# A decoder layer with routed experts: gated rows written to their tokens, against rows kept by slot and gathered

## Chip, cores and metric

The kernel runs on 1 core of one Trainium2 chip. The metric is the device time of a run in microseconds (us); lower is better.

## What is computed

The layer takes 64 sequences of 128 tokens with 256 features (8192 tokens) and applies three residual blocks with a normalization after each: a mixer, a cross attention, and a feed-forward block with routed experts. The change touches only the last one and the routing that prepares it. Cut to what matters:

```python
shared = silu(xf @ sg) * (xf @ su) @ sd                     # every token
top_scores, top_idx = top_k(masked, K)                      # K = 4 of E = 32 experts
gates = softmax(top_scores, axis=-1)
capacity = int(N / E * K * 1.25)                            # 1280 rows per expert
pos = cumsum(onehot, axis=0)[arange(N * K), flat_e] - 1     # place in the expert's list
keep = pos < capacity
h = silu(einsum('ecd,edh->ech', buf, wg)) * einsum('ecd,edh->ech', buf, wu)
out_e = einsum('ech,ehd->ecd', h, wd)
gathered = out_e[flat_e, minimum(pos, capacity - 1)]
contrib = gathered * (flat_g * keep)[:, None]
routed = zeros_like(xf).at[tok].add(contrib)
x = layernorm(x + shared + routed)
```

## The kernel before, in words

Five engines run side by side: TensorE (PE), VectorE (DVE), ScalarE (ACT), GpSimd (POOL), and SyncE (SP), which issues plain transfers. Each runs its own program in order, and semaphores tie them together. There is no scheduler: the order on each engine is the order in which the code is written. The stages follow one another with a barrier between them: `setup_stage`, `mixer_stage`, `attention_stage`, `expert_stage` (tiles `e_`), `combine_stage` (tiles `f_`). Matrix products of the last two stages are split into a high and a low part of each operand, three matmuls for each product (L1207).

**Attention stage.** Sixteen groups of 512 tokens. Behind the attention, DVE chooses four experts for each token and computes `slot_i`, the row of `slot_token` for each (token, choice); pairs beyond capacity get a row out of bounds. POOL scatters the token's number there, 16 indirect transfers to a group (L969), and raises `tok` by 512 for the next one (L976). DVE also keeps gates (`k.gate`) and row numbers (`k.slot`) of all tokens in SBUF. SP fills `expert_rows` in DRAM with zeros, 2560 KB to a group. A list of work items is made at the end: 256 rows of one expert each, 92 of them here.

**Expert stage.** Item w uses buffers w % 2. SP loads the token numbers of item w+2 (`load_tok`, L1292), its gate and up weights (`load_up`), the down weights of w+1 (`load_down`), and then stores the rows of item w-1 into `expert_rows` (`store`, L1313). POOL gathers the 256 input rows of item w+2 with two indirect transfers (`gather`, L1354) and makes the low part of the down weights (`down_low`, L1363). PE runs `up(w)`, the transposes of item w+1 (`turn`, L1394), `down(w-1)`. DVE copies the finished product out of PSUM (`copied`, L1545). Engines walk a loop of 79 rounds of two items and skip the rounds that have none.

**Combine stage.** Sixteen groups of 512 tokens. PE runs `up(g)` (48 matmuls of 512 columns), `turn(g+1)` (8 transposes) and `down(g)` (48 matmuls of 256 columns). `down(g)` waits for the last low part of the hidden rows (L1759). POOL gathers four expert rows for each token, 16 indirect transfers to a group (`fetch`, L1639), and computes the inverse deviation (`rstd`, L1646 and L1648). DVE adds the rows one group later, 16 multiply-adds to a group (`adds`, L1770), and normalizes (L1778 to L1788).

Of the kernel before, what the change touches and what calls it, by code (L numbers as in the profile page):

```python
# [90 lines left out]
def setup_stage(nc, k, dram):  # L91

    with ExitStack() as ctx:
# [12 lines left out]
        with nc.Block() as block:  # L106
# [12 lines left out]
            def _(pool):  # L119
# [17 lines left out]
                pool.iota(k.tok[:], pattern=[[T, TG]], base=0, channel_multiplier=1).then_inc(iot, 1)  # L137
# [400 lines left out]
def attention_stage(nc, k, dram):  # L538
# [6 lines left out]
    with ExitStack() as ctx:  # L545
# [32 lines left out]
        pos, kept, posc = p.sb("pos", [P, TG, K]), p.sb("kept", [P, TG, K]), p.sb("posc", [P, TG, K])  # L578
        base = p.sb("base", [P, TG, K])
        far, slot_i = p.sb("far", [P, TG, K]), p.sb("slot_i", [P, TG, K], I32)  # L580
        blank = p.sb("blank", [RT, (SLOTS + SETW) // RT], I32)
        zero_rdy, filled = p.sem("zero_rdy"), p.sem("filled")
# [15 lines left out]
        posc_rdy, hand_rdy, scattered, tok_rdy = p.sem("posc"), p.sem("hand"), p.sem("scattered"), p.sem("tok")  # L598
# [66 lines left out]
        with nc.Block() as block:  # L665
            @block.sync
            def _(sp):
# [8 lines left out]
                FILLED = SLOTS // NG  # L676

                sp.wait_ge(blank_rdy, 1)
                sp.dma_start(k.slot_tok.rearrange("(p n) a -> p (n a)", p=RT), blank[:]).then_inc(blanked, 16)
                sp.wait_ge(zero_rdy, 1)  # L680

                def store(g):
                    sp.dma_start(k.out_d[bass.ds(g * FILLED, FILLED), :].rearrange("(p n) d -> p n d", p=P),
                                 zero[:, None, :].to_broadcast([P, FILLED // P, D])).then_inc(filled, 16)
# [21 lines left out]
                sp.wait_ge(filled, DMA + 16 * NG)  # L706
                sp.wait_ge(blanked, DMA + 16)
# [188 lines left out]
            def _(pool):  # L896
                pool.memset(zero[:], 0.0).then_inc(zero_rdy, 1)
                begin(pool, xs_rdy, xb_rdy, ve_rdy, rs_rdy, rxs_rdy, nms_rdy, nrm_rdy, tok_rdy, mask_rdy)
                pool.memset(blank[:], 0).then_inc(blank_rdy, 1)
                pool.memset(r_half[:], 0.5).then_inc(half_rdy, 1)  # L900
# [54 lines left out]
                def scatter(r, batches, paced):  # L955


                    for j in batches:
                        if j == 0:
                            pool.wait_ge(slot_rdy, ONE + r + 1)  # L960
                            pool.wait_ge(tok_rdy, ONE + r)
                            pool.wait_ge(blanked, DMA + 16)
# [5 lines left out]
                        for q in range(K):  # L968
                            pool.indirect_dma_start(  # L969
                                k.slot_tok, bass.IndirectOffsetOnAxis(ap=slot_i[:, j, q:q + 1], axis=0),  # L970
                                k.tok[:, j:j + 1], None, bounds_check=SLOTS - 1, oob_is_err=False)\
                                .then_inc(scattered, 16)
                    if TG - 1 in batches:
                        pool.wait_ge(scattered, 16 * TG * K * (r + 1))
                        apart(pool, k.past_pool)
                        pool.tensor_scalar(k.tok[:], k.tok[:], float(GW), None, ALU.add).then_inc(tok_rdy, 1)  # L976
# [38 lines left out]
            def _(dve):  # L1015
                begin(dve, a_out[0], nb_rdy, rden_rdy, n_rdy, h_rdy, stat_rdy, mv_rdy, ot_rdy,
                      step, slot_rdy, posc_rdy, dif_rdy)
# [64 lines left out]
                def place(r):  # L1082
# [7 lines left out]
                    then(dve.tensor_tensor(dif[:], ex[:], er[:, :, None].to_broadcast([P, TG, K]), ALU.mult))  # L1090
# [120 lines left out]
def expert_stage(nc, k, dram):  # L1211
# [3 lines left out]
    with ExitStack() as ctx:  # L1215
# [57 lines left out]
        with nc.Block() as block:  # L1273
            @block.sync
            def _(sp):
# [40 lines left out]
                def item(w, a):  # L1316
# [3 lines left out]
                    if at_least(w, 1):  # L1320
                        store(w - 1, 1 - a)
# [576 lines left out]
```

## Time and profile before

| | |
|---|---|
| median of 3 runs | 2421.14 us (2417.51 to 2422.02) |
| the profiled execution: time, span | 2423.74 us, 2422.2 us |
| busy: PE, DVE, ACT, POOL | 88%, 65%, 50%, 56% |
| expert stage, from the first gather to the last copy | 1139.3 to 2001.9 us |
| combine stage, from its first instruction to the end | 2004.7 to 2422.2 us |

Times in the trace count from the span's start. Busy shares are averages over stages with different limits, so each stage is read by itself. A DMA's issue on SP is short; the time to landing is given apart. "issue" as a reason for idle time means that the profile shows nothing that the engine waited for.

### The profile page before, as it was taken

What the parts mean: (1) busy time and instruction counts of PE and PEld (TensorE: products, weight loads), DVE (VectorE), ACT (ScalarE), POOL (GpSimd) and SP (SyncE); (2) the same over time, 40 slices, a digit from 0 to 9 for tenths busy, and PEclk for the clock granted to TensorE, in tenths of its full rate; (3) what the DMA queues carried; (4) which work ended last, traced back from release to release, by engine and by line L of the source; (5) the groups of instructions that cost most, each with busy time, mean ns of one, the idle gap of its engine ahead of it and who ended that gap; (6) DMA issues with size and microseconds to landing.
All of it is one profiled execution on the core that took longest, in us unless ns stands there. A gap on an engine that the chain in (4) does not pass through costs nothing. (4 is left out here: it accounts for less than half of the span.)

```text
span 2422.2 us, 51520 instructions
## 1 busy us (share of the span) xinstructions
PE 2123.5 (88%) x13848; PEld 1722.7 (71%) x13848; DVE 1574.4 (65%) x3953; ACT 1211.0 (50%) x3430; POOL 1351.9 (56%) x1648
## 2 busy tenths in 40 slices
PE   6999699999999999830999999999999956878884
PEld 3555356666666666530999999999999955777774
DVE  4666335667667666632777777777777743766666
ACT  2555245444455445410777777777777742222221
POOL 3666303456655655555555555555555535777775
PEclk9999899999999999955999999999999987989897
DMA  4000112322411321301666666666667643444343
GB/s 127 33 0 0 46 50 78 98 62 59 117 59 59 107 69 59 101 13 58 209 236 239 237 234 228 237 242 228 238 227 243 238 143 126 132 121 136 119 137 91
DMA packets 240146, 317.12 MB, mean 131 GB/s; under 512 B 38073, under 2 KB 161761, under 8 KB 240098
## 3 DMA queue, kind: packets, MB, share of 16 engines
q1 hardware_dynamic: 210594, 258.19, 31.9%
q0 software_dynamic: 29504, 58.37, 8.2%
q8 instruction: 21, 0.34, 0.1%
q14 instruction: 27, 0.22, 0.0%
HBM read 233.34 MB, written 83.14 MB: 131 GB/s over the span
## 5 line engine op out<-in xcount | busy, mean ns | idle before, releaser
L969 POOL DMA_INDIRECT slot_token<-tok,a_slot_i x256 | 267.9, 1047 | 231.0 <-issue 95.6
L1354 POOL DMA_INDIRECT e_xg<-x_rows,e_tok x188 | 197.4, 1050 | 346.2 <-DMA e_tok<-slot_token 188.1
L1639 POOL DMA_INDIRECT f_row<-expert_rows,f_idx x256 | 273.9, 1070 | 89.9 <-issue 76.7
L1532 DVE TENSOR_TENSOR e_hid<-e_sg,e_u 128x256 f32<-128x256 f32 x368 | 155.1, 421 | 133.3 <-PE e_u L1207 106.7
L1482 ACT ACTIVATE e_sg<-e_g 128x256 f32<-128x256 f32 x368 | 141.2, 384 | 179.6 <-PE e_g L1207 179.6
L852 ACT ACTIVATE a_prob<-a_s,a_ntop 128x128 f32<-128x128 f32 x512 | 180.2, 394 | 0.8 <-DVE a_ntop L1149 0.5
L1730 ACT ACTIVATE f_sg<-f_g 128x512 f32<-128x512 f32 x64 | 38.2, 597 | 222.1 <-PE f_g L1207 222.1
L1363 POOL TENSOR_TENSOR e_wd1l<-e_raw_d,e_wd1h 128x256 fp32r<-128x256 f32 x184 | 130.4, 742 | 30.0 <-ACT e_wd1h L1461 29.8
L1207 PE MATMUL f_d<-f_wdh,f_hth 128*128 128x256 f32 x256 | 85.6, 334 | 63.6 <-DVE f_htl L1759 63.6
L1363 POOL TENSOR_TENSOR e_wd0l<-e_raw_d,e_wd0h 128x256 fp32r<-128x256 f32 x184 | 130.9, 743 | 7.3 <-ACT e_wd0h L1461 6.4
L1207 PE MATMUL e_d<-e_wd1h,e_ht1h 128*128 128x256 f32 x368 | 108.3, 294 | 24.5 <-issue 24.5
L783 PE MATMUL a_o<-a_wo,a_ot 128*128 128x256 f32 x512 | 125.6, 390 | 4.2 <-DVE a_ot L1179 4.2
L736 PE MATMUL a_a<-a_wv,a_ct 96*128 96x512 f32 x256 | 120.9, 606 | 6.9 <-ACT a_rxt L837 5.5
L726 PE MATMUL a_a<-a_xt,a_wq 128*128 128x512 f32 x256 | 122.7, 614 | 0.8 <-ACT a_xt L837 0.8
L732 PE MATMUL a_a<-a_ct,a_wk 96*128 96x512 f32 x256 | 120.5, 605 | 0.0
L852 ACT ACTIVATION_READ_ACCUMULATOR a_prob<-a_s,a_ntop 128x1 f32 x512 | 120.5, 235 | 0.0
L1545 DVE COPY e_out<-e_d 128x512 f32<-128x512 f32 x92 | 63.6, 692 | 87.4 <-PE e_d L1207 87.4
L1133 DVE TENSOR_TENSOR x<-a_o,x 128x256 f32 (+1 forms) x64 | 27.2, 425 | 133.5 <-PE a_o L783 133.5
L1207 PEld LDWEIGHTS f_d<-f_wdh,f_hth 128*128 128x128 f32 x256 | 59.9, 234 | 67.6 <-DVE f_htl L1759 38.7
L1207 PE MATMUL e_d<-e_wd0h,e_ht0h 128*128 128x256 f32 x368 | 107.4, 292 | 0.0
L1770 DVE SCALAR_TENSOR_TENSOR f_res<-f_row,gate,f_res 128x256 f32<-128x256 f32 x256 | 106.6, 480 | 0.1
L783 PEld LDWEIGHTS a_o<-a_wo,a_ot 128*128 128x128 f32 x512 | 95.4, 197 | 15.2 <-DVE a_ot L1179 4.4
(262 smaller groups left out, 7522.9 us busy)
## 6 DMA issues: line engine op xcount, KB each, us to landing
e_raw_g<-in_eg SPq DMA_DIRECT2D x94, 512.0 KB
e_raw_u<-in_eu SPq DMA_DIRECT2D x94, 512.0 KB, 4.2
e_raw_d<-in_ed SPq DMA_DIRECT2D x93, 512.0 KB, 5.0
expert_rows<-a_zero SPq DMA_DIRECT2D x16, 2560.0 KB, 11.8
expert_rows<-e_out SPq DMA_DIRECT2D x92, 256.0 KB, 2.2
x<-in_x SPq DMA_DIRECT2D x16, 512.0 KB, 3.4
x_rows<-x SPq DMA_DIRECT2D x16, 512.0 KB, 3.4
f_xs<-x_rows SPq DMA_DIRECT2D x16, 512.0 KB, 4.8
```

Of the source, the lines that this page charges most:

```text
L726: last = pe.matmul(out[:], wq[:, c, m * P:(m + 1) * P], xt[:, c, :], start=(c == 0), stop=(c == DC - 1))
L732: last = pe.matmul(out[:], wk[:, c, m * P:(m + 1) * P], ct[par][:, c, :], start=(c == 0), stop=(c == 1))
L736: last = pe.matmul(out[:], ct[par][:, c, m * T:(m + 1) * T], wv[:, c, :], start=(c == 0), stop=(c == 1))
L783: last = pe.matmul(bank_o[:, 0:D], ot[:, m, :], wo[:, m, :], start=(m == 0), stop=(m == IC - 1))
L852: last = act.activation(prob[b % 2][:, h, :], bank_s[r][:, m * T:(m + 1) * T], ACT.Exp, bias=ntop[b % 2][:, h:h + 1], accum_out=den[b % 2] ...
L969: pool.indirect_dma_start(k.slot_tok, bass.IndirectOffsetOnAxis(ap=slot_i[:, j, q:q + 1], axis=0), k.tok[:, j:j + 1], None, bounds_check=S ...
L1207: last = pe.matmul(out, a, b, start=(n == 0 and t == 0), stop=(n == len(chunks) - 1 and t == 2))
L1354: pool.indirect_dma_start(xg[a][:, n, :], None, k.x2_d, bass.IndirectOffsetOnAxis(ap=tok[a][:, n:n + 1], axis=0))\
L1363: pool.tensor_tensor(wd[par][1][:, m, :], raw_d[par][:, m, :], wd[par][0][:, m, :].bitcast(F32), ALU.subtract).then_inc(dl_rdy, 1)
L1482: act.activation(sg[m % 2][:], bank_g[m % 2][:, 0:SETW], ACT.Silu).then_inc(sg_rdy, 1)
L1532: dve.tensor_tensor(hid[m % 2][:], sg[m % 2][:], bank_u[m % 2][:, 0:SETW], ALU.mult)\
L1639: pool.indirect_dma_start(row[a][:, j, q, :], None, k.out_d[0:SLOTS, :], bass.IndirectOffsetOnAxis(ap=idx[a][:, j, q:q + 1], axis=0))\
```

## The change

1. An entry of `slot_token` has three numbers: the token, the row `4 * token + choice` of a new DRAM tensor `part_rows`, and the gate's bits. Blank entries point to spare rows. DVE no longer writes `k.gate` and `k.slot`. The wait for `tok_rdy` on DVE stands four operations earlier.
2. In the expert stage DVE scales each row by its gate as it leaves PSUM (`gated`, two operations for one). POOL writes the rows of item w-2 to `part_rows` with two indirect transfers (`put_rows`). SP loads the entries of item w once more (`load_dest`), after the rows of item w-2 have landed, since these used the same buffer. SP no longer stores rows.
3. In the combine stage SP loads the four rows of each token plainly (`fetch_part`, 2 MB to a group). POOL adds them and the input (`parts`, four additions of 128x1024) in place of its 16 gathers. DVE's 16 multiply-adds are gone. PE runs `down(g-1)` in group g, with hidden rows in two buffers. DVE normalizes group g-2 in group g.
4. SP's zeros now fill `part_rows`, 2048 KB to a group, and 256 spare rows of `x2_rows`.

```diff
 # expert stage, SP
-                def store(w, a):
+                def load_dest(w, a, i):
                     start = slots(w)
-                    sp.wait_ge(out_rdy, OUT + NP * (w + 1))
-                    sp.dma_start(k.out_d[bass.ds(start, SETW), :].rearrange("(p n) d -> p n d", n=TI), out[a][:])\
-                        .then_inc(stored[a], 16)
-
-                def item(w, a):
+                    if at_least(i, 1):
+                        sp.wait_ge(put[a], 16 * TI * i)
+                        apart(sp, k.past_sp)
+                    sp.dma_start(dest[a][:], k.slot_tok[bass.ds(start, SETW), :].rearrange("(p n) a -> p n a", n=TI))\
+                        .then_inc(dest_in[a], 16)
+
+                def item(w, a, i):
                     load_tok(w + 2, a)
                     load_up(w + 2, a)
                     load_down(w + 1, 1 - a)
-                    if at_least(w, 1):
-                        store(w - 1, 1 - a)
+                    load_dest(w, a, i)
 # expert stage, POOL
+                def put_rows(w, a):
+                    pool.wait_ge(out_rdy, OUT + TI * (w + 1))
+                    apart(pool, k.past_pool)
+                    for n in range(TI):
+                        pool.indirect_dma_start(k.part_d, bass.IndirectOffsetOnAxis(ap=dest[a][:, n, 1:2], axis=0),
+                                                out[a][:, n, :], None).then_inc(put[a], 16)
+
+                def item(w, a, i):
+                    gather(w + 2, a, i + 1)
+                    if at_least(w, 2):
+                        put_rows(w - 2, a)
+                    down_low(w, a)
 # expert stage, DVE
-                def copied(w, a, i):
...
+                def gated(w, a, i):
+
+                    dve.wait_ge(dest_in[a], DMA + 16 * (i + 1))
+                    gate = dest[a][:].bitcast(F32)
+                    for n in range(TI):
+                        if n % 2 == 0:
+                            dve.wait_ge(d_done, ONE + NP * w + n // 2 + 1)
+                        dve.tensor_scalar(out[a][:, n, :], bank_d[a][0:RT, (n % 2) * D:(n % 2 + 1) * D],
+                                          gate[:, n, 2:3], None, ALU.mult).then_inc(out_rdy, 1)
 # combine stage, SP
+                def group(g, a, i):
+                    if at_least(g, 2):
+                        store(g - 2, a)
+                    if not isinstance(g, int) or g + 2 < NG:
+                        sp.wait_ge(acc_rdy, ONE + 4 * (g + 1))
+                        apart(sp, k.past_sp)
+                        fetch(g + 2, a)
+                        fetch_part(g + 2, a)
 # combine stage, POOL
+                    for n, (out, x, y) in enumerate(((to, part[a][:, :, 0, :], part[a][:, :, 1, :]),
+                                                     (both, part[a][:, :, 2, :], part[a][:, :, 3, :]),
+                                                     (to, to[:], both[:]), (to, to[:], xs[a][:]))):
+                        if n >= 2:
+                            pool.wait_ge(acc_rdy, ONE + 4 * g + n)
+                        pool.tensor_tensor(out[:], x, y, ALU.add).then_inc(acc_rdy, 1)
 # combine stage, PE
+                def group(g, a, i):
+                    up(g)
+                    if not is_last(g):
+                        turn(g + 1, 1 - a, i + a)
+                    if at_least(g, 1):
+                        down(g - 1, 1 - a)
```

SP in the loop of the expert stage, from the end of one item into the next (`e_tok`: token numbers, `e_out`: finished rows, `e_dest`: the entries loaded again, `e_put`: counts rows that have landed in `part_rows`). Before:

```order
L1312 REGISTER_ALU
L1313 ISA [waits e_out]
L1313 DMA expert_rows<-e_out 128x512
L1285 ISA
L1285 TENSOR_LOAD plan
L1285 ISA x2
L1290 ISA
L1292 REGISTER_ALU [waits e_t_done]
L1292 DMA e_tok<-slot_token 128x2
```

And now:

```order
L1321 REGISTER_ALU
L1323 ISA [waits e_put0]
L1323 DMA e_dest<-slot_token 128x6
L1293 ISA
L1293 TENSOR_LOAD plan
L1293 ISA x2
L1298 ISA
L1300 ISA [waits e_t_done]
L1300 DMA e_tok<-slot_token 128x6
```

Ahead of the load of token numbers stood a store that waits for DVE (`e_out`); now there stands a load that waits for rows that POOL has written. `TENSOR_LOAD plan` reads an item's first row from the list of items.

POOL in the same loop, one item (`e_xg`: gathered input rows, `e_wd0l`: low part of the down weights). Before:

```order
L1350 ISA
L1351 ISA [waits e_t_done]
L1354 DMA e_xg<-x_rows,e_tok 128x256 [waits e_tok_in0]
L1354 DMA e_xg<-x_rows,e_tok 128x256
L1362 ISA [waits e_d_done]
L1363 TENSOR_TENSOR e_wd0l<-e_raw_d,e_wd0h 128x256 [waits e_dh]
```

And now:

```order
L1358 ISA
L1359 ISA [waits e_t_done]
L1362 DMA e_xg<-x_rows,e_tok 128x256 [waits e_tok_in0]
L1362 DMA e_xg<-x_rows,e_tok 128x256
L1375 ISA
L1378 DMA part_rows<-e_out,e_dest 41216x256 [waits e_out]
L1378 DMA part_rows<-e_out,e_dest 41216x256
L1370 ISA [waits e_d_done]
L1371 TENSOR_TENSOR e_wd0l<-e_raw_d,e_wd0h 128x256 [waits e_dh]
```

Two indirect writes stand behind the two gathers of the same item, and the gathers still wait for the token numbers that SP loads.

## Rows read from the trace of the kernel before

**Rows 1.** The page's busy time of PE: us, share, instructions.
```profile
PE 2123.5 (88%) x13848; PEld 1722.7 (71%) x13848; DVE 1574.4 (65%) x3953; ACT 1211.0 (50%) x3430; POOL 1351.9 (56%) x1648
```

**Rows 2.** Stretch, length; busy PE, PEld, DVE, ACT, POOL; clock; DMA share; GB/s.
```profile
450.00:700.00 250.00, 244.42 (x1495) 158.20 (x1494) 171.49 (x520) 124.14 (x463) 149.85 (x193) 1.00 0.28 72
1300.00:1500.00 200.00, 200.00 (x1705) 200.00 (x1704) 153.38 (x336) 150.18 (x404) 112.66 (x137) 1.00 0.69 237
2140.00:2240.00 100.00, 80.15 (x413) 70.08 (x412) 67.47 (x164) 23.33 (x41) 75.89 (x78) 0.88 0.43 130
```

**Rows 3.** SP's queue in the expert stage, in order: start, duration, issue.
```profile
1481.33 0.37 SPq L1313 DMA_DIRECT2D expert_rows<-e_out  x1
1482.71 0.35 SPq L1292 DMA_DIRECT2D e_tok<-slot_token  x1
...
1490.25 0.37 SPq L1313 DMA_DIRECT2D expert_rows<-e_out  x1
1492.48 0.36 SPq L1292 DMA_DIRECT2D e_tok<-slot_token  x1
...
1500.56 0.35 SPq L1292 DMA_DIRECT2D e_tok<-slot_token  x1
```

**Rows 4.** POOL in the same stretch, in order; idle before in brackets.
```profile
1485.30 1.43 POOL L1354 DMA_INDIRECT e_xg<-x_rows,e_tok  x1 [2.83 <-issue]
1487.04 1.17 POOL L1354 DMA_INDIRECT e_xg<-x_rows,e_tok  x1 [0.30 <-issue]
1488.22 2.82 POOL L1363 TENSOR_TENSOR e_wd1l<-e_raw_d,e_wd1h 128x256 fp32r<-128x256 f32 x4
1494.98 1.01 POOL L1354 DMA_INDIRECT e_xg<-x_rows,e_tok  x1 [3.94 <-DMA e_tok<-slot_token]
...
1503.08 0.95 POOL L1354 DMA_INDIRECT e_xg<-x_rows,e_tok  x1 [2.76 <-issue]
```

**Rows 5.** The tile `e_xg`: landing of its transfers.
```profile
DMA to landing us min/median/max: 2.7/4.6/6.4
```

**Rows 6.** DMA issues: count, KB each, median us to landing.
```profile
expert_rows<-e_out SPq DMA_DIRECT2D x92, 256.0 KB, 2.2
```

**Rows 7.** POOL at the end of the last scatter, in order.
```profile
1129.25 0.97 POOL L969 DMA_INDIRECT slot_token<-tok,a_slot_i  x1 [0.30 <-issue]
1131.53 0.22 POOL L976 TENSOR_SCALAR tok<-tok 128x4 int32<-128x4 int32 x1 [1.31 <-DMA slot_token<-tok,a_slot_i]
```

**Rows 8.** PE in the combine stage: pieces of the chain and one instruction row.
```profile
2038.50 5.95 PE f_d L1207 x48
2047.23 1.40 PE f_g L1207 x6
2141.82 1.09 PE L1669 MATMUL f_t<-ident,f_xs 128*128 128x128 f32 x8
```

**Rows 9.** POOL in the combine stage at the start of two groups.
```profile
2134.01 0.19 POOL L1633 COPY f_idx<-slot 128x16 int32 x1
...
2158.72 0.19 POOL L1633 COPY f_idx<-slot 128x16 int32 x1
```

**Rows 10.** PE after its wait in the combine stage.
```profile
2147.84 0.58 PE L1207 MATMUL f_d<-f_wdh,f_hth 128*128 128x256 f32 x1 [4.92 <-DVE f_htl L1759]
```

**Rows 11.** The start of the combine stage: ACT and PE.
```profile
2016.66 1.06 ACT L1737 ACTIVATE f_wgh<-f_raw_g 128x1024 fp32r<-128x1024 f32 x1 [45.02 <-DMA f_raw_d<-in_sd]
2022.58 0.79 PE L1207 MATMUL f_g<-f_xth,f_wgh 128*128 128x512 f32 x1 [11.98 <-DVE f_xtl L1754]
```

**Rows 12.** DVE at the end of the span.
```profile
2413.84 1.40 DVE L1778 BATCH_NORM_STATS2 f_stat<-f_res 128x6 f32<-128x256 f32 x4
```

**Rows 13.** POOL's groups: count, busy us, mean ns, idle before.
```profile
L1363 POOL TENSOR_TENSOR e_wd0l<-e_raw_d,e_wd0h 128x256 fp32r<-128x256 f32 x184 | 130.9, 743 | 7.3 <-ACT e_wd0h L1461 6.4
L906 POOL TENSOR_TENSOR x<-x,bout 128x1024 f32 x10 | 23.6, 2359 | 0.0
L1639 POOL DMA_INDIRECT f_row<-expert_rows,f_idx x256 | 273.9, 1070 | 89.9 <-issue 76.7 <-POOL f_idx L1633 13.2
```

More of the change, by code:

```diff
@@ L975, in scatter @@
                         apart(pool, k.past_pool)
-                        pool.tensor_scalar(k.tok[:], k.tok[:], float(GW), None, ALU.add).then_inc(tok_rdy, 1)
+                        for n, step_by in enumerate((GW, GW * K)):
+                            last = pool.tensor_scalar(entry[:, :, :, n], entry[:, :, :, n], float(step_by), None, ALU.add)
+                        last.then_inc(tok_rdy, 1)
                 def around(g):
@@ L1368, in first @@
                     gather(1, 1, 0)
-                    gather(2, 0, 1)
-                    down_low(0, 0)
-                    gather(3, 1, 1)
-                    down_low(1, 1)
+                    item(0, 0, 0)
+                    item(1, 1, 0)
                 def again(i):
-                    gather(2 * i + 2, 0, i + 1)
-                    down_low(2 * i, 0)
-                    gather(2 * i + 3, 1, i + 1)
-                    down_low(2 * i + 1, 1)
+                    item(2 * i, 0, i)
+                    item(2 * i + 1, 1, i)
                 used, last = rounds(pool, first, again)
+                put_rows(last - 1, 0)
+                put_rows(last, 1)
                 pool.wait_ge(x_in[1], 16 * TI * (used + 1))
                 apart(pool, k.past_pool)
+                for a in range(2):
+                    pool.wait_ge(put[a], 16 * TI * used)
+                    apart(pool, k.past_pool)
             @block.tensor
@@ L1592, in combine_stage, with at_least, groups, is_last @@
         sg_rdy, hid_rdy, d_done, sum_rdy = p.sem("sg"), p.sem("h"), p.sem("d_done"), p.sem("sum")
-        add_rdy, stat_rdy, mv_rdy, ve_rdy = p.sem("add"), p.sem("stat"), p.sem("mv"), p.sem("ve")
+        stat_rdy, mv_rdy, ve_rdy = p.sem("stat"), p.sem("mv"), p.sem("ve")
         rs_rdy, res_rdy = p.sem("rs"), p.sem("res")
-        stored = [p.sem(f"stored{i}") for i in range(2)]
         out_d = dram["out"].rearrange("b t d -> t b d")
-        x2_rows = k.x2_d.rearrange("(b t) d -> t b d", t=T)
+        x2_rows = k.x2_d[0:B * T, :].rearrange("(b t) d -> t b d", t=T)
+        part_rows = k.part_d[0:B * T * K, :].rearrange("(b t q) d -> t b (q d)", t=T, q=K)
+        def at_least(g, n):
+            return not isinstance(g, int) or g >= n
+        def groups(eng, group):
+            group(0, 0, 0)
+            group(1, 1, 0)
+            with eng.Fori(1, NG // 2 - 1) as i:
+                group(2 * i, 0, i)
+                group(2 * i + 1, 1, i)
+            group(NG - 2, 0, NG // 2 - 1)
+            group(NG - 1, 1, NG // 2 - 1)
+        def is_last(g):
+            return isinstance(g, int) and g == NG - 1
         with nc.Block() as block:
@@ L1822, in _ @@
                     dve.tensor_tensor(w[1][:], raw[i][:], w[0][:].bitcast(F32), ALU.subtract).then_inc(wl_rdy, 1)
-                turned(0)
-                group(0, 0, 0)
-                group(1, 1, 0)
-                with dve.Fori(1, NG // 2 - 1) as i:
-                    group(2 * i, 0, i)
-                    group(2 * i + 1, 1, i)
-                group(NG - 2, 0, NG // 2 - 1)
-                group(NG - 1, 1, NG // 2 - 1)
-                for q in range(K):
-                    adds(NG - 1, 1, NG // 2 - 1, q)
+                groups(dve, group)
+                moments(NG - 2, 0)
+                normed(NG - 2, 0)
+                summed(NG - 1, 1, NG // 2 - 1)
                 moments(NG - 1, 1)
```

317 lines of the change are left out of this document (148 added, 169 removed).

## The prediction, made before the changed kernel was run

> **What bounds the kernel now.** I read the page first: PE is busy for 88% of the span [rows 1]. That is an average over stages, so the next view is busy time by stretch [rows 2]. In the attention stretch PE works 244.42 of 250 us. In the expert stage it works 200.00 of 200 us at the full granted clock (1.00, 2.4 GHz), with POOL at 112.66 and DVE at 153.38. In the combine stage it works only 80.15 of 100 us at a mean clock of 0.88, with POOL at 75.89 busy us. So PE sets the first two, and something else sets the third.
>
> For the expert stage I want the time of one item. SP's issues repeat once an item: two stores stand 1490.25 - 1481.33 = 8.92 us apart [rows 3]. There are 92 items (the stores' count, [rows 6]).
>
> For the combine stage, POOL starts two successive groups at 2134.01 and 2158.72, 24.71 us apart [rows 9]. Its 16 gathers take 1.07 us each [rows 13] and 0.30 us between two ([rows 4] show such a gap). With `rstd`, the copy and their waits that is the whole period. PE also has a wait of its own there, for the last low part of the hidden rows, 4.92 us before `down` [rows 10], and needs far less: 8 blocks of six matmuls at 1.40, transposes of 1.09 and 5.95 for 48 matmuls of `down` are 18.2 us [rows 8].
>
> **Combine stage, the gain.** POOL's 16 gathers leave; four additions of 128x1024 come. The nearest row has 2.359 us for this shape; the dearest one by element has 0.743 us for 256 columns, so 2.97 us for 1024 [rows 13]. Four are 9.4 to 11.9 us, and with some 3 us for `rstd` and waits POOL needs 12.5 to 15 us of a group. DVE loses 16 multiply-adds. `down(g-1)` needs hidden rows that were finished a group before, so the wait of 4.92 us has nothing to wait for. Loads are 3 MB a group (2 of parts, 0.5 in, 0.5 out): 165 GB/s at 18.2 us, under the 237 GB/s that the expert stage moves [rows 2]. PE therefore becomes the bound, at 18.2 us: 16 groups are 291 us.
>
> The start: the weights have landed at 2016.66 and PE starts at 2022.58 [rows 11]. Now no gathers run beside the weights' load, and the first turned rows (two subtractions on DVE) are made ahead of them. I estimate 4 us less in all, so a start at 2018.5. The slow clock at the start costs some 2.5 us (rows 11 show 0.79 for a first matmul). PE ends at 2018.5 + 291 + 2.5 = 2312. Behind it come the last half of the sum (0.9) and what runs today from the statistics to the end, 2422.2 - 2413.84 = 8.4 us [rows 12]. End: 2321, so **-101 us**.
>
> **Expert stage, the loss.** DVE's two scaled copies for one copy, and POOL's two writes for each item, are small beside idle time: POOL is busy 5.0 us of an item's 8.92 [rows 2] and 2 x 1.3 us more still fit. As busy time the change costs nothing here. What it adds is a closed loop of waits. Follow it through the two orders above:
>
> 1. SP issues the token numbers of w+3. POOL's gather of w+3 starts 2.5 us later: 1482.71 to 1485.30, 1492.48 to 1494.98, 1500.56 to 1503.08 [rows 3, 4].
> 2. Two gathers: 1.74 us from the first to the second [rows 4], 1.3 where nothing disturbs (1.01 and the gap of 0.30), so 1.4; then 1.17 + 0.30 to the next issue, 1.4. Sum 2.8.
> 3. POOL's first write of w-1 stands behind them (its rows have long been ready), 1.3 us to the second.
> 4. SP waits until both have landed, L from the start of the second. No row shows this transfer. Below: the last scatter of 4-byte entries starts at 1129.25 and the wait for it ends at 1131.53, 2.3 us [rows 7]. Above: gathers of such rows land 4.6 us after issue at the median, plus 0.2 for SP: 4.8. Their minimum is 2.7 [rows 5]. The two writes start about 4 us behind the first gather, when the item's weights have nearly landed, so I take a lightly loaded one: **L = 3.0**.
> 5. SP issues `load_dest(w+1)`, and the token numbers of w+4 follow as they follow the store today: 1.38 us within a round, 2.23 across the loop's end (1490.25 to 1492.48) [rows 3]; mean 1.8.
>
> Sum: 2.5 + 2.8 + 1.3 + 3.0 + 1.8 = **11.4 us** for one turn, and each turn makes exactly one item. Before, step 4 was a wait for DVE's copy of the product just finished, and PE's own 8.92 us set the rate. In the loop are also queued: `load_up` and `load_down` behind SP's wait, which PE needs only an item later, and POOL's `down_low` (2.82 us [rows 4]) behind the writes, which is over before the next token numbers land. PE sees about 2.5 us of waits per item, in two parts: for the input rows before `turn`, and for the low down weights before `down`.
>
> SP's wait starts with item 2, so 90 turns: (11.4 - 8.92) x 90 = **+223 us**. With L = 2.3 it is +160, with L = 4.8 +385.
>
> The Trainium skill, page DMA: Bandwidth & Descriptors, section Anatomy of one DMA — SWDGE (gpsimd) path, puts a transfer's cost at 2.0 us plus bytes over 436 GB/s, mostly the receipt from the target memory, behind about 1 us for making the descriptors. For 128 KB that is an estimate of 3.3 us for L, and the sum by it would be 250 in place of 223.
>
> **The seam.** Behind the last product stand two scaled copies, two writes and L in place of a copy and a store that lands in 2.2 us [rows 6]: some +2 us.
>
> **Attention stage.** Scattered entries have 12 bytes in place of 4, in as many transfers. The earlier wait for `tok_rdy` and a second small addition on POOL (0.22 us each, [rows 7]) may hold DVE for parts of a us in a group, against three small operations less. PE is the bound there at 98% and DVE has 171 busy of 250 us [rows 2]: 0, within 5 us. SP's zeros are less (2048 KB for 2560) and hidden either way.
>
> **The sum.** 223 - 101 + 2 = +124 us. The profiled execution took 2423.74 us, 2.6 above the median; on the median of 2421.14 I forecast 2545 us. The bounds of L give 2482 to 2707.
>
> **Rivals.**
> - *The loop hides; faster.* The expert stage keeps 8.92 us an item and only the combine gain remains: 2421 - 101 + 2 = 2322 us. For it speaks POOL's 44% of idle time there. Place: SP's wait for the writes. Price: 90 us for each us of a turn. It decides where the turn comes to 8.92 + 99 / 90 = 10.0 us, so at L = 1.6; the shortest landing in the trace is 2.3. Chance 0.08.
> - *The clock falls.* PE's waits of 1 to 2 us in each item could bring the granted clock down to 1.2 GHz. In the combine stage a wait of 4.92 us stands ahead of matmuls at 0.58 for 256 columns and a mean clock of 0.88 [rows 2, 10]. Wholly at half the clock, an item would cost up to 17.8 us and the run 2421 + 800 - 99 = 3120. Below 11.4 / 8.92, so with up to 28% more PE time, the loop hides it. The waits are shorter than the one that is seen to do it, so 0.05. The Trainium skill, page TensorE: Matmul & The Clock Gate, section HAM oscillation — how this bites in real kernels, describes this for matmul bursts with waits for DMA between them; no row of this stage shows it yet.
> - *The combine stage finds another bound.* POOL's additions, the order store, load, parts on SP, or the load of the inputs for `turn` could hold a group at 20 to 22 us: 30 to 60 us more, 2575 to 2605. It lies within the range; 0.12. The Trainium skill, page GPSIMD Engine Reference, section Specifications, says that GpSimd shares its SBUF interface with VectorE and that DVE instructions with two SBUF inputs contend; by that the additions are dearer, and the 0.743 us row, taken beside such instructions, is the bound used above.
> - *A longer loop*, with writes that land after 4.8 us or more: above 2707; 0.05.
>
> **How the numbers follow.** The loop with L from 2.3 to 4.8 and PE-bound combine has 0.70, the same loop with a slower combine 0.12, a longer loop 0.05, the fallen clock 0.05, the hidden loop 0.08. The range of 2475 to 2710 holds the first two. Only the hidden loop is faster; a result within 0.2% (5 us, about what a measurement of this kernel can tell from no change) needs L near 1.6: 0.01. Faster 0.08, same 0.01, slower 0.91.
>
> **What the changed profile would show.** Right: SP's queue waits for the landing of `part_rows`, its issues of token numbers stand 11.4 us apart on average in the expert stage, PE has two short waits an item, its clock stays near 1.00, and the expert stage is some 220 us longer. In the combine stage PE is busy almost without a break and a group takes 18.2 us. Wrong: issues 8.9 us apart (the loop hides), a landing of the writes far from 3.0, a PE clock well under 1, or groups over 19 us with PE waiting for POOL or for a load.

## Result and profile after: slower, 2546.5 us

The changed kernel took 2546.52 us (median of 4 runs, 2543.96 to 2548.92), and the kernel before 2419.37 us in the same measurement (4 runs, 2417.51 to 2422.02). The ratio is 1.0526, with a 95% interval of 1.0513 to 1.0539. The forecast was 2545 us.

First the page of the changed kernel, busy time of PE, and then busy time by stretch: length, busy PE, PEld, DVE, ACT, POOL, clock, DMA share, GB/s.

```profile
PE 2161.0 (85%) x13848; PEld 1739.8 (68%) x13848; DVE 1656.4 (65%) x3741; ACT 1213.5 (48%) x3430; POOL 1517.8 (60%) x1643
...
450.00:700.00 250.00, 244.37 (x1503) 159.60 (x1503) 167.92 (x494) 125.84 (x468) 154.49 (x201) 1.00 0.21 65
1300.00:1500.00 200.00, 170.61 (x1333) 165.20 (x1332) 149.47 (x278) 118.94 (x316) 135.73 (x141) 0.96 0.54 187
2300.00:2400.00 100.00, 100.00 (x588) 88.65 (x587) 75.41 (x142) 30.63 (x55) 67.23 (x36) 1.00 0.50 178
```

Against [rows 2] the attention stretch stands as it was. In the expert stage PE now idles 15% of the time, and the DMA rate fell from 237 to 187 GB/s. In the combine stage PE has no idle time left. So the two big stages have changed places: PE set the expert stage before, and sets the combine stage now.

SP's queue in the expert stage (start, duration, issue), and then what SP waited for there (us in total, times, longest):

```profile
1490.59 0.35 SPq L1300 DMA_DIRECT2D e_tok<-slot_token  x1
1491.88 0.38 SPq L1307 DMA_DIRECT2D e_raw_g<-in_eg  x1
1492.45 0.38 SPq L1310 DMA_DIRECT2D e_raw_u<-in_eu  x1
1493.75 0.37 SPq L1316 DMA_DIRECT2D e_raw_d<-in_ed  x1
1499.71 0.34 SPq L1323 DMA_DIRECT2D e_dest<-slot_token  x1
1501.07 0.35 SPq L1300 DMA_DIRECT2D e_tok<-slot_token  x1
...
1510.59 0.34 SPq L1323 DMA_DIRECT2D e_dest<-slot_token  x1
1512.42 0.35 SPq L1300 DMA_DIRECT2D e_tok<-slot_token  x1
...
2188.90 0.35 SPq L1300 DMA_DIRECT2D e_tok<-slot_token  x1
...
SPq L60 <- DMA part_rows<-e_out,e_dest: 499.7, 90, 7.0
```

POOL beside it (start, duration, instruction; idle before in brackets):

```profile
1497.04 0.99 POOL L1378 DMA_INDIRECT part_rows<-e_out,e_dest  x1 [0.30 <-issue]
1498.06 4.08 POOL L1371 TENSOR_TENSOR e_wd0l<-e_raw_d,e_wd0h 128x256 fp32r<-128x256 f32 x4
1503.46 0.99 POOL L1362 DMA_INDIRECT e_xg<-x_rows,e_tok  x1 [1.31 <-issue]
1504.75 0.96 POOL L1362 DMA_INDIRECT e_xg<-x_rows,e_tok  x1 [0.30 <-issue]
1506.02 1.01 POOL L1378 DMA_INDIRECT part_rows<-e_out,e_dest  x1 [0.30 <-issue]
1507.33 0.99 POOL L1378 DMA_INDIRECT part_rows<-e_out,e_dest  x1 [0.30 <-issue]
```

One can walk the loop in these rows. Token numbers are issued at 1501.07. The gather starts 2.39 us later, the first write 2.56 after that (1506.02), the second 1.31 later (1507.33), and SP is past its wait 3.26 later (1510.59). The next token numbers follow after 1.83. This turn took 11.35 us, and every part of it starts when the part before it ends. SP waited for the writes 90 times, which is every item but the first two. From the load of item 5's numbers at 1181.63 to the last one at 2188.90 there are 88 items, which is 11.45 us an item.

In the combine stage, POOL at the start of three groups:

```profile
2308.39 0.23 POOL L1684 TENSOR_SCALAR f_ve<-f_mv 128x4 f32<-128x4 f32 x1 [5.15 <-DVE f_mv L1832]
...
2325.92 0.23 POOL L1684 TENSOR_SCALAR f_ve<-f_mv 128x4 f32<-128x4 f32 x1 [5.25 <-DVE f_mv L1832]
...
2327.24 2.53 POOL L1702 TENSOR_TENSOR f_acc<-f_part 128x1024 f32<-128x1024 f32 x1
2329.73 2.84 POOL L1702 TENSOR_TENSOR f_both<-f_part 128x1024 f32<-128x1024 f32 x1
2332.64 2.74 POOL L1702 TENSOR_TENSOR f_acc<-f_acc,f_both 128x1024 f32<-128x1024 f32 x1
2335.46 2.74 POOL L1702 TENSOR_TENSOR f_acc<-f_acc,f_xs 128x1024 f32<-128x1024 f32 x1
2343.46 0.23 POOL L1684 TENSOR_SCALAR f_ve<-f_mv 128x4 f32<-128x4 f32 x1 [5.25 <-DVE f_mv L1832]
```

A group takes 17.53 us against 24.71 in [rows 9], and POOL has over 5 us to spare in each. PE has none; the chain of waits there is PE alone (start, length, piece):

```profile
2311.20 1.36 PE f_g L1213 x6
...
2313.92 0.87 PE f_t L1722 x8
2314.79 5.76 PE f_d L1213 x48
```

By stages: the attention stage ends 1.2 us later (first gather at 1140.5 for 1139.3). From that gather to the combine stage's first instruction (at 2233.2) it is 1092.7 us for 865.4, so +227.3. The combine stage takes 312.9 us for 417.5, so -104.6. Together +123.9, which is the difference of the two spans (2546.1 and 2422.2).

### The profile page after: what moved, and what is told of

Same layout as the page of the kernel before. It is cut to its first block and busy times, and to the rows that moved or that the text cites. A ratio compares the mean times of both kernels' runs of the same rounds, so it can differ in the third digit from the quotient of the medians.

```text
span 2546.1 us, 51191 instructions
## 1 busy us (share of the span) xinstructions
PE 2161.0 (85%) x13848; PEld 1739.8 (68%) x13848; DVE 1656.4 (65%) x3741; ACT 1213.5 (48%) x3430; POOL 1517.8 (60%) x1643
## 5 line engine op out<-in xcount | busy, mean ns | idle before, releaser
L980 POOL DMA_INDIRECT slot_token<-a_entry,a_slot_i x256 | 270.3, 1056 | 245.6 <-issue 95.6
L1378 POOL DMA_INDIRECT part_rows<-e_out,e_dest x184 | 195.0, 1060 | 79.1 <-issue 66.7
L1569 DVE TENSOR_SCALAR e_out<-e_d,e_dest 128x256 f32<-128x256 f32 x184 | 80.3, 478 | 149.2 <-PE e_d L1213 148.5
L1371 POOL TENSOR_TENSOR e_wd0l<-e_raw_d,e_wd0h 128x256 fp32r<-128x256 f32 x184 | 172.4, 965 | 7.7 <-ACT e_wd0h L1483 6.7
L1371 POOL TENSOR_TENSOR e_wd1l<-e_raw_d,e_wd1h 128x256 fp32r<-128x256 f32 x184 | 168.9, 946 | 6.0 <-ACT e_wd1h L1483 4.9
L1544 DVE TENSOR_TENSOR e_ht1l<-e_hid,e_ht1h 128x256 fp32r<-128x256 f32 x184 | 134.7, 753 | 0.0
L1213 PEld LDWEIGHTS e_d<-e_wd0h,e_ht0h 128*128 128x128 f32 x368 | 78.4, 213 | 74.0 <-issue 73.8
L1544 DVE TENSOR_TENSOR e_ht0l<-e_hid,e_ht0h 128x256 fp32r<-128x256 f32 x184 | 123.6, 692 | 0.0
L1213 PE MATMUL e_g<-e_xth,e_wg1h 128*128 128x256 f32 x368 | 106.1, 288 | 19.9 <-DVE e_xtl L1539 19.9
L1213 PEld LDWEIGHTS e_d<-e_wd1h,e_ht1h 128*128 128x128 f32 x368 | 74.0, 201 | 71.1 <-issue 71.0
```

The lines of the kernel that those rows point to most:

```text
L980: pool.indirect_dma_start(k.slot_tok, bass.IndirectOffsetOnAxis(ap=slot_i[:, j, q:q + 1], axis=0), entry[:, j, q, :], None, bounds_check=S ...
L1213: last = pe.matmul(out, a, b, start=(n == 0 and t == 0), stop=(n == len(chunks) - 1 and t == 2))
L1371: pool.tensor_tensor(wd[par][1][:, m, :], raw_d[par][:, m, :], wd[par][0][:, m, :].bitcast(F32), ALU.subtract).then_inc(dl_rdy, 1)
L1378: pool.indirect_dma_start(k.part_d, bass.IndirectOffsetOnAxis(ap=dest[a][:, n, 1:2], axis=0), out[a][:, n, :], None).then_inc(put[a], 16)
L1544: dve.tensor_tensor(ht[a][1][:, m, :], hid[m % 2][:], ht[a][0][:, m, :].bitcast(F32), ALU.subtract).then_inc(hl_rdy, 1)
```

## Experiments

Twelve runs of ten different kernels followed (the kernels before and after among them), in four measurements on three chips, each with its own runs of the kernel before. In the first of them that kernel took 2580.05 us (13 runs, 2570.27 to 2591.89) with a mean clock near 0.917; in the other three it took 2418.65, 2419.97 and 2423.61 us, as in the measurement of the result. No profile of it on that chip exists. It ran unchanged with a profile in two later measurements, on other chips, and took its usual time:

*The kernel before, twice.* 

> The kernel before, unchanged, for its profile beside the experiments: in their measurement it took 2580 us, in the first one 2419. Theory: one stage of it alone is longer, and the changed kernel does not have it. First candidate, its combine stage with 256 indirect gathers on POOL (1.07 us each in the first profile): if they take longer there, the group is over 30 us in place of 24.7, and the stage over 500 us in place of 417. Rival: the expert stage is longer, 10.6 us an item in place of 8.92, by the clock or by its loads. Second rival: all stages are longer by the same share, as a lower clock would make them. If this run takes 2420 us again, the difference is one of the chip or of the moment and stays open.

 Measured: 2420.38 us. 

> The kernel before once more, for its profile beside the runs of this measurement. If it takes some 2580 us as in one measurement before, its stages by stretch say where the 160 us are: in the combine stage alone, by a group over 30 us or a lower clock there, or in the expert stage. If it takes 2419 us, that difference stays open.

 Measured: 2424.98 us. So the 160 us stay open, and ratios of the first measurement are not used below; its kernels are compared with one another and by their periods. The changed kernel itself was not run in that measurement: it took 2546.52 and 2549.31 us in two others.

### Is it the loop? The destinations an item later

Item w's destination entries are loaded at the end of item w+1, so SP waits for writes that were issued an item earlier. DVE needs them only after the product of item w, an item after the old place. Not shown are two small transfers on POOL ahead of the stage, which let the first waits pass.

```diff
...
-                    load_dest(w, a, i)
+                    if at_least(w, 1):
+                        load_dest(w - 1, 1 - a, i if a else i - 1)
...
+                load_dest(last, 1, used - 1)
```

> The changed kernel, with one difference in the expert stage: SP loads the entries of item w-1, not of item w, at the end of its item w, so its wait for landed rows is for writes that POOL issued one item earlier. The work on every engine stays the same, but for two small transfers ahead of the stage. Theory of the closed loop (SP's wait, token numbers, gathers, writes, landing): the turn of about 11.4 us now makes two items, 5.7 us each, PE's 8.92 us set the rate again, the expert stage is about 225 us shorter, and the time is 2320 to 2345 us. Rival, POOL and the transfers are too busy with two writes more in an item: the work is unchanged, so the time stays within 20 us of the changed kernel's 2546.5. Rival, DVE's scaled copies wait for their entries: these now land later, so the time is the same or higher.

Measured: 2357.05 us (2355.1 to 2360.23), some 190 us under the changed kernel as the theory of the loop has it, but 12 us above its range; an item takes 9.09 us. SP's largest wait of this kind in the whole trace (us in total, times, longest) is now for PE's transposes, and none for a landing of `part_rows` is left:

```profile
SPq L60 <- PE e_t L1421: 110.5, 59, 4.9
```

It was run once more:

> The experiment with the destinations loaded an item later, once more, beside a kernel before that takes its usual time. In its profile POOL works without a pause in the expert stage: 1.46 + 1.19 + 1.23 + 1.17 for the four indirect issues, 2.81 for the low parts and some 1.1 between them, 8.98 us an item, and PE needs 8.92. Theory (the loop is open, and POOL's own work is now level with PE): 2350 to 2365 us, 0.97 to 0.98 of the kernel before and 185 to 200 us less than the changed kernel, wherever it runs. Rival: its 2357 us belong to the chip of that measurement, and it takes 2400 us or more.

Measured: 2335.62 us (2334.97 to 2337.92), ratio to the kernel before 0.9644 (0.9622 to 0.9665), and an item takes 8.98 us. That is 14 us under the range expected of this run. The changed kernel took 2549.31 us (below), so one load moved by one item takes 214 us away. That is the whole loss and more. Both kernels write and gather the same rows with the same instructions; but for the two small transfers, only what SP waits for differs. Busy time and clock in the same stretch as above, and POOL:

```profile
1300.00:1500.00 200.00, 200.00 (x1694) 200.00 (x1693) 154.82 (x356) 149.08 (x400) 162.12 (x180) 1.00 0.70 234
...
1491.28 1.46 POOL L1367 DMA_INDIRECT e_xg<-x_rows,e_tok  x1 [0.16 <-issue]
1493.04 1.19 POOL L1367 DMA_INDIRECT e_xg<-x_rows,e_tok  x1 [0.30 <-issue]
1494.54 1.23 POOL L1383 DMA_INDIRECT part_rows<-e_out,e_dest  x1 [0.30 <-issue]
1496.07 1.17 POOL L1383 DMA_INDIRECT part_rows<-e_out,e_dest  x1 [0.30 <-issue]
1497.26 2.82 POOL L1376 TENSOR_TENSOR e_wd1l<-e_raw_d,e_wd1h 128x256 fp32r<-128x256 f32 x4
1500.23 1.48 POOL L1367 DMA_INDIRECT e_xg<-x_rows,e_tok  x1 [0.16 <-issue]
```

PE is at 200 of 200 us again, as in [rows 2]. In this item POOL has no gap longer than 0.30 us: its own work fills it (1491.28 to 1500.23), and of the 3.9 us of an item that it had free before almost nothing is left. Which of the two sets the 8.98 us was not separated. PE has no wait in the trace between 1200 and 1900 us, while POOL waits there 24 times for ACT, 26.0 us in all, which speaks for PE.

### Another way to open it: the writes ahead of the gathers

```diff
-                    gather(w + 2, a, i + 1)
                     if at_least(w, 2):
                         put_rows(w - 2, a)
+                    gather(w + 2, a, i + 1)
```

> The changed kernel, with POOL's two writes of item w-2 ahead of the two gathers of item w+2 in place of behind them. SP's program is unchanged. Theory of the closed loop: the writes no longer stand behind gathers that need the token numbers of the same turn. The chain from one write to the next is 1.3 + 3.3 (landing) + 1.6 (SP) + 2.5 (token numbers) + 2.6 (gathers) + 3 to 4 (low part of the weights), about 14.5 us, for two items, so 7.2 us an item: PE sets the rate, 2320 to 2350 us. Rival, POOL or transfers too busy: within 20 us of 2546.5, as nothing is removed. If the landing of the writes alone were to blame, it would also stay.

Measured: 2364.68 us (2355.9 to 2379.22), in the same measurement as the 2357.05, so some 8 us behind it. An item takes 9.34 us. That is above the range of 2320 to 2350. The writes of item w no longer wait for the token numbers just issued, so that the loop runs through two items and no longer holds each. SP still waits for landings between 1200 and 1900 us (total, times, longest):

```profile
SPq L60 <- DMA part_rows<-e_out,e_dest: 202.8, 60, 5.4
```

What sets the last 0.4 us above PE's 8.92 is not shown. The longer loop is one candidate, but POOL waits only 14 times for token numbers there, 7.9 us in all. POOL itself is another: in the stretch from 1508.12 to 1526.15 it works through two items without a longer gap than 0.31 us, at 9.02 us an item.

Both edits at once:

> The destinations loaded an item later and the writes ahead of the gathers, both at once. Theory (POOL without a pause at 8.98 us an item is the bound once the loop is open, so its order does not matter): within 5 us of the destinations loaded later alone, 2350 to 2365 us. Rival (what is left above PE's 8.92 us an item is still a wait for a landing, which earlier writes shorten): 10 to 20 us less, 2335 to 2345 us. Second rival: the gathers start 2.7 us later than they could, PE waits for its input rows, and it is 5 to 20 us longer.

Measured: 2335.70 us (2334.11 to 2338.2), beside 2335.62 for the first edit alone. With the loop open, the order on POOL does not matter: the two times differ by 0.08 us. By its absolute range (2335 to 2345) the rival would have it, but the run beside it came out 14 us under its range too, and the rival wanted 10 to 20 us between the two. That POOL's own work is the bound, as the first theory says in brackets, does not follow: PE is as full.

### What does a us in the loop cost?

An addition of 128x512 on POOL (1.05 us and 0.17 behind it), whose result nobody uses, stands between the gathers and the writes (in the loop) or behind the writes (outside it).

```diff
...
+                def more_work(w):
+                    pool.wait_ge(more, ONE + w)
+                    pool.tensor_tensor(spare[:], k.keep[:], k.keep[:], ALU.add).then_inc(more, 1)
...
                     gather(w + 2, a, i + 1)
+                    more_work(w)
                     if at_least(w, 2):
                         put_rows(w - 2, a)
```

> The changed kernel with one more addition on POOL in each item, 128x512 into a spare tile (about 1.27 us by such rows of the kernel before), put between the gathers and the writes, so inside the supposed loop. Theory of the closed loop: each us in it costs 90 us, so +105 to +125 us, 2650 to 2670. Rival, POOL's busy time sets the rate: POOL has idle time of 3 us an item, so the same small change as for the run with the work outside the loop. Rival, transfers or DVE set the rate: no change.

> The same additional POOL work as in the run with the work inside the loop, but behind the writes, where SP waits for their landing at the same time. Theory of the closed loop: it is hidden, at most 30 us more through the low part of the down weights coming later, for which PE already waits; 2546 to 2580. Rival, POOL's busy time sets the rate: +105 to +125 us here too.

Measured: 2583.08 us (10 runs, 2579.14 to 2587.47) in the loop, 2554.47 us (2545.25 to 2563.97) outside. The place matters, as the loop says: the second expectation holds, the first does not. In the loop the addition costs 28.6 us more than outside it (and 34 to 37 us more than the changed kernel took on other chips), about a third of the 105 to 125 us expected. SP's and POOL's rows of the kernel with the addition in the loop show where the rest went:

```profile
1495.63 0.37 SPq L1317 DMA_DIRECT2D e_raw_d<-in_ed  x1
1502.61 0.35 SPq L1324 DMA_DIRECT2D e_dest<-slot_token  x1
...
1497.45 1.05 POOL L1359 TENSOR_TENSOR e_spare<-keep 128x512 f32<-128x512 f32 x1
1498.66 1.00 POOL L1383 DMA_INDIRECT part_rows<-e_out,e_dest  x1 [0.17 <-issue]
1499.97 0.97 POOL L1383 DMA_INDIRECT part_rows<-e_out,e_dest  x1 [0.30 <-issue]
```

From the second write to SP's next issue it is 2.64 us here, where the rows of the changed kernel had 3.26. Over the turns between 1200 and 1900 us (59 here, 61 in the changed kernel) the mean is 2.77 us in place of 3.44, and from the first gather to the first write 3.62 in place of 2.64. Of the 0.98 us added, 0.67 is given back, and the turn grows from 11.41 to 11.74 us; 90 times that is 30 us. What hardly moves is the time from SP's issue of the down weights to its next load of destinations: 6.97 us here and 6.78 there. That suggests that the writes land late because of the weights moved beside them, and not by a time of their own. (The two kernels are from different chips, so the shift of a few tenths is less sure than the 28.6 us; the next run tests it.)

### The weights behind the landing

SP waits for the writes and loads the destinations before it issues the three weight loads, so nothing large is on its way when the writes are.

```diff
                     load_tok(w + 2, a)
+                    load_dest(w, a, i)
                     load_up(w + 2, a)
                     load_down(w + 1, 1 - a)
-                    load_dest(w, a, i)
```

> Expert stage: SP waits for the writes and loads the destination rows before it issues the three weight loads of the item, not behind the token numbers and the first weight load; all else as changed. Theory (the writes land late because the item's own 1.5 MB of weights is on its way with them): with the weights issued behind them the wait from the second write to their landing falls from 3.4 to 2.2 to 2.6 us, but the three issues now stand between that and the next token numbers (1.6 becomes 4 to 5 us), the turn is 12.5 to 13.5 us and the kernel 90 to 180 us longer. Rival (the landing of 1 KB rows written by index takes 3.4 us whatever else is moved): the interval stays at 3.3 to 3.5 and the turn is 13.5 to 14.5 us, 190 to 280 us longer.

Measured: 2906.48 us (2904.05 to 2916.06), ratio 1.2009 (1.1986 to 1.2031). An item takes 15.5 us. The landing term went from 3.44 to 2.66 on average (46 turns, 2.64 to 2.69), just above the theory's 2.2 to 2.6 and well under the rival's 3.3 to 3.5. That answers the question of the run: a landing takes 2.66 us without the weights beside it and 0.78 us more with them, as in the changed kernel. But both expectations were too low, 12.5 to 14.5 us for the turn and at most 280 us for the whole, where 357 us came. The three issues stand between destinations and token numbers, 4.65 us for 1.60, as expected. What neither had is that the token numbers now land behind 1.5 MB of weights: from their issue to the gather it is 4.04 us on average in place of 2.43. The rows show both, and then the stretch and PE's waits between 1200 and 1900 us:

```profile
1492.00 0.38 SPq L1307 DMA_DIRECT2D e_raw_g<-in_eg  x1
...
1495.26 0.34 SPq L1300 DMA_DIRECT2D e_tok<-slot_token  x1
1506.53 0.34 SPq L1323 DMA_DIRECT2D e_dest<-slot_token  x1
...
1499.74 0.99 POOL L1362 DMA_INDIRECT e_xg<-x_rows,e_tok  x1 [7.90 <-issue]
...
1300.00:1500.00 200.00, 143.34 (x987) 140.66 (x985) 90.39 (x208) 84.10 (x234) 90.37 (x105) 0.83 0.41 137
...
PE e_g L1213 <- ACT e_sg L1504: 196.0, 45, 5.4
```

This run also shows the rival in which the clock falls. With waits of up to 5.4 us before `up`, PE's mean clock is 0.83 in the expert stage. With the changed kernel's waits of at most 3.5 us it is 0.96. The time is still the loop's: its terms, 4.04 + 2.83 + 1.31 + 2.66 + 4.65, are the 15.5 us of the turn.

### The combine stage: the gathers or the later product?

*The changed kernel once more, for comparison.* 

> The changed kernel, unchanged, beside the experiments. In the first measurement it took 2547 us and the kernel before 2419. Theory: its stages do not depend on what made the kernel before slow in the second measurement, so 2530 to 2560 us, an item of 11.4 us and a group of 17.5 us. Rival: it is slower by the same share, some 2700 us.

 Measured: 2549.31 us (2546.37 to 2553.1), ratio 1.0538 (1.0516 to 1.0561), within the expected 2530 to 2560.

The order of PE is undone: the down product runs in its own group again.

```diff
                 def group(g, a, i):
                     up(g)
                     if not is_last(g):
                         turn(g + 1, 1 - a, i + a)
-                    if at_least(g, 1):
-                        down(g - 1, 1 - a)
+                    down(g, a)
...
-                down(NG - 1, 1)
```

> Undoes one part: in the combine stage the down product of a group runs behind the hidden rows of the same group, not a group later. Theory (PE is the bound of this stage and the later product takes its wait for the hidden rows away): PE waits 4 to 5 us in each of 16 groups for the last low part of the hidden rows, the group goes from 17.5 to 21.5 to 24 us, with a lower clock on top, so 60 to 110 us more than the changed kernel. Rival (POOL's gathers alone set the group before; with them gone the order on PE does not matter): PE waits, but the group stays near 17.5 to 18.5 us, 0 to 15 us more.

Measured: 2648.76 us (2647.68 to 2658.49), 99 us more, inside the theory's range, but not for its reason. A group takes 24.4 to 25.7 us. PE's wait of 5.4 us ended with a sum, not with the hidden rows (PE's waits from 2300 to 2500 us, total, times, longest):

```profile
PE f_d L1213 <- DVE f_res L1816: 43.1, 8, 5.5
```

DVE takes the sum of group g-1 late in group g, and it empties the bank that `down(g)` needs. That is a wait of my own making, so the sum was moved too:

```diff
 # DVE, the end of a group
-                    if at_least(g, 1):
-                        summed(g - 1, 1 - a, i - 1 + a)
-                    if at_least(g, 2):
-                        normed(g - 2, a)
+                    if at_least(g, 1):
+                        normed(g - 1, 1 - a)
+                    summed(g, a, i)
 # POOL
-                    if at_least(g, 2):
-                        rstd(g - 2)
                     parts(g, a, i)
+                    if at_least(g, 1):
+                        rstd(g - 1)
...
```

> As the run with the down product in its own group, and the sum of a group taken behind its product in the same group too, statistics and norm one group later, as before the change; POOL makes its four additions ahead of the inverse deviation. In the run before, PE's wait of 5.4 us in each group ended by the sum of the group before, which DVE takes only behind the turned rows: 1.9 us of it are that order, and some 3.5 us are the wait for the last low part of the hidden rows. Theory (half of the gain of this stage is the later product, not the gathers): PE waits 3.5 to 5 us a group for the hidden rows, the clock is 0.88 to 0.92 and a group takes 22.5 to 24.7 us, so 80 to 115 us more than the changed kernel's 2549. Rival (the wait was the late sum alone, and the gathers' absence gives the gain): a group of 17.5 to 19.5 us, 0 to 35 us more.

Measured: 2637.69 us (2630.3 to 2639.79), ratio 1.0878 (1.085 to 1.0906), which is 88 us more than the changed kernel and inside the theory's range. PE, a stretch of it, and POOL's `ve` in two groups:

```profile
2386.09 0.58 PE L1213 MATMUL f_d<-f_wdh,f_ht1h 128*128 128x256 f32 x1 [3.39 <-DVE f_ht1l L1806]
2409.95 0.57 PE L1213 MATMUL f_d<-f_wdh,f_ht0h 128*128 128x256 f32 x1 [3.40 <-DVE f_ht0l L1806]
...
2300.00:2500.00 200.00, 172.81 (x882) 153.67 (x881) 150.19 (x209) 47.40 (x86) 92.45 (x51) 0.87 0.40 142
...
2379.60 0.22 POOL L1684 TENSOR_SCALAR f_ve<-f_mv 128x4 f32<-128x4 f32 x1 [10.33 <-DVE f_mv L1829]
2403.56 0.23 POOL L1684 TENSOR_SCALAR f_ve<-f_mv 128x4 f32<-128x4 f32 x1 [10.47 <-DVE f_mv L1829]
```

A group takes some 23.9 us with no gather in it and POOL idle over half the time. Of the 6.3 us over 17.53, 3.4 are PE's wait, and about 3 are the clock: PE is busy 20.6 us of a group (172.81 of 200) where 17.5 do at 1.00. By the ratios, the undone order costs 1.0878 - 1.0538 = 3.4% of 2419, that is 82 us (give or take 9, by the two intervals) of the stage's gain of 105. So PE's own chain bound the stage before nearly as tightly as POOL's gathers did. That the gathers alone would have held a group at 24.7 us, with PE's order changed, was not run: it is read from 16 gathers at 1.07 and 0.30 us apart, 21.9 us of the group [rows 9, 13]. The trace of the kernel before supports it: from 2134.01 to 2158.72 POOL works without a longer pause than 0.82 us, and that one is for its own copy.

## Why the prediction was right

**The loop, +223.** Right in mechanism and in sum: 11.45 us an item for 11.4, and +227.3 us for the stage and its seam for 225. That it is the loop, and no busy engine, the load moved by one item shows. Its terms, as means over the 61 turns between 1200 and 1900 us: token numbers to gather 2.43 for 2.5, gathers 2.64 for 2.8, between the writes 1.31 for 1.3, landing 3.44 for 3.0, destinations to token numbers 1.60 for 1.8. They sum to 11.4, as the turns do. That the sum was met so closely is in part luck: the landing was 0.44 us longer than forecast, which alone is 40 us, and three other terms together were 0.43 shorter. The Trainium skill, page DMA: Bandwidth & Descriptors, section Anatomy of one DMA — SWDGE (gpsimd) path, gives 2.0 us plus bytes over 436 GB/s, which for 128 KB is an estimate of 2.3 us; the 3.3 in the prediction has 1 us for the descriptors on top, which that section does not add. The runs show 2.66 without the weights beside the writes, between the two, and 3.44 with them.

**"Price: 90 us for each us of a turn."** This step failed, in the rival of the hidden loop. Each us of a turn does cost 90 us, but the terms are not independent: an addition of 1.2 us put ahead of the writes made the turn only 0.33 us longer, because the landing became 0.67 us shorter. In the same way, the reason for L = 3.0 (writes that start when the weights have nearly landed) named the right neighbour and took too little for it: 0.34 us over the 2.66 without weights, where 0.78 was measured.

**The combine stage, -101.** Measured -104.6. The group took 17.53 us for 18.2, since the pieces of PE's chain are a little shorter there than in [rows 8] (1.36 for 1.40, 0.87 for 1.09, 5.76 for 5.95); PE started 13.5 us into the stage for 17.9 before, so 4.4 us earlier for 4. The four additions took 10.85 us, inside 9.4 to 11.9. The dear end of that was said to be taken beside DVE instructions with two SBUF inputs; of the 313 rows behind it between 1200 and 1900 us only 41 are, and the others lie beside operations that read PSUM. What the text did not price is how close the second bound was. It called POOL's gathers and what goes with them "the whole period", which the trace bears out, and set PE's 18.2 us beside it; but with its wait and the lower clock that comes with it, PE's own chain took 23.9 us in the run without gathers. The gain needed both edits: with the gathers gone, the later product is worth 82 of the 105 us, and without it their absence brought little more than 20.

**The clock.** Forecast near 1.00, measured 0.96 to 0.97 in the expert stage. No cost of it is seen, as the text says, since the loop covers it: PE is busy 170.61 of 200 us. Its waits came to 1.7 us an item for the 2.5 forecast, because its own work took 9.7 us of an item in place of 8.92, and nearly all of them were for the low parts of the down weights and of the input rows; the input rows themselves held it for 7.8 us in all between 1200 and 1900 us.

**Extra busy time on POOL "costs nothing".** Nearly true of the changed kernel: 1.2 us more on POOL outside the loop cost 5 to 8 us, between different chips. POOL's low parts took 946 to 965 ns for 743, and PE waited for them 105.5 us in all. With the loop open POOL has next to nothing to spare. **Attention:** +1.2 us, within the 5. **SP's waits:** 90, as counted.

## What to carry to other kernels

When a buffer's reuse makes a queue wait for its own later output, follow the wait around until it comes back to its start, and sum the loop: it can set the rate while no engine is busy. Count how many items the loop spans; moving the waiting load one item later spreads the waits over two items, and here that made a slower change 3.6% faster than the kernel it replaced. And when a stage has one engine that is full and another that waits, undo one part at a time before naming the bound: here, as far as the runs and the trace show, both had to go.

## What the hardware showed that was not expected

**DVE and POOL slow each other.** DVE at the low parts of the hidden rows in the changed kernel, while POOL worked at its own from 1498.06 to 1502.14 (4.08 us for four, against 2.82 in [rows 4]), and then the same instruction in the kernel with the later load, at a moment when POOL was issuing transfers:

```profile
1498.59 0.95 DVE L1544 TENSOR_TENSOR e_ht1l<-e_hid,e_ht1h 128x256 fp32r<-128x256 f32 x1
1499.68 0.42 DVE L1554 TENSOR_TENSOR e_hid<-e_sg,e_u 128x256 f32<-128x256 f32 x1
```

```profile
1494.81 0.42 DVE L1549 TENSOR_TENSOR e_ht1l<-e_hid,e_ht1h 128x256 fp32r<-128x256 f32 x1
```

Two SBUF tiles in, one out: 0.95 us beside POOL's low parts and 0.42 apart from them. Over the changed kernel's trace from 1200 to 1900 us, 83 of these lie wholly beside POOL's low parts, with a median of 0.95 us, and 146 apart from them, at 0.42. `e_hid`, which reads one of its inputs from PSUM, took 0.42 in the same moment. The Trainium skill, page GPSIMD Engine Reference, section Specifications, says that the two share an SBUF interface, with contention for DVE instructions with two SBUF inputs. The trace agrees for the hidden rows and adds the price, but not every such instruction pays it: the low parts of the up weights (128x512, both inputs in SBUF) took 0.68 us at the median both beside POOL's low parts (37 of them) and apart.

**An issue of an indirect transfer is not a fixed cost.** Between 1200 and 1900 us a gather takes POOL 1.22 us on average in the kernel with the later load (1.46 in the rows above) and 0.98 in the changed one, a write 1.15 for 1.06. More traffic goes beside it, 234 GB/s for 187, but that is not the only candidate: in the combine stage of the kernel before (from 2050 us), all 65 gathers that POOL issued while DVE was idle took at most 0.96 us, and all 16 over 1.3 us lie beside DVE's low parts of hidden rows, which have both inputs in SBUF. No run separates the two.

**A small load behind large ones waits for them.** The token numbers' way to the gather grew from 2.43 to 4.04 us when 1.5 MB of weights were issued ahead of them.
